# Attention and mixture of experts on one core: three PSUM banks shared in turn by scores and side work, a fourth bank for the maxima

## The chip, the cores and the metric

The kernel runs on one core of a Trainium2 chip. The metric is the device time of one execution in microseconds (us). TensorE is called PE below, its weight loads PEld, VectorE is DVE, ScalarE is ACT, GpSimd is POOL, and SyncE, which issues most transfers, is SP.

## What is computed

The input is 16 images of 128 channels and 32x32 pixels. Each image is normalised over its channels, goes through an attention of 8 heads of 16 features over 1024 tokens, is projected and added to the input. Then each token is normalised again and goes to the two best of 16 experts.

```python
xs = reshape(x, (B, T, C))                      # B = 16, T = 1024, C = 128
q, k, v = einsum('btc,hcd->bhtd', xs, Wq), ...  # H = 8 heads, D = 16
att = softmax(einsum('bhtd,bhsd->bhts', q, k) / sqrt(D))
x = x + reshape(concat_heads(att @ v) @ Wproj + bproj)
t = tokens(x)
t = t + experts(top2_gating(layernorm(t)))      # E = 16, capacity 256, hidden 512
```

## The kernel before

It has two phases. The attention of the 16 images takes the first three quarters of the time; then 272 blocks of 128 rows go through the experts. The change concerns the first phase.

**Slots.** An image is 128 slots. A slot is one matmul of scores, with 128 keys as rows and 512 queries as columns of one head (`score_unit`, L1515), and the exponential of that tile on ACT (`exp_unit`, L818). The softmax needs a row maximum before it. So every slot also has one matmul for the maxima (`max_unit`, L1491), with 128 queries as rows and 512 keys as columns, which DVE reduces along the row (`take_max`, L978). PE is 45 slots ahead with these (`LEAD`): in slot u it issues the maximum matmul of slot u + 45 and then the score matmul of slot u. An image has four stages of 32 slots. After the last maximum of a stage, DVE splits the 128x16 maxima into two parts, PE transposes them into rows (`rows_of_maxima`, L1501, in the slots with u % 32 == 24), ACT copies the rows out (L850), and two transfers put them below the queries, where the score matmul subtracts them.

**Weighing.** After every fourth score PE multiplies four finished probability tiles with the values (`weigh`, L1532, eight matmul instructions). It waits for the exponential of the last of the four. In a stage it comes after the scores of slots 2, 7, 10, 14, 18, 22, 26 and 30. At the end of a stage DVE divides the result in four small steps (slots 4 to 7 of the next stage); the first weighing of a stage, in slot 7, also waits for the first of them (L1010).

**Side work.** The order in which PE does the rest is written out by hand by the slot. For the image after: two groups of transposes of x (after the scores 1 and 5, L1463), four projections to queries and keys (33, 41, 44, 48, L1471), and two groups of projections to values (51, 54, L1477). For the image before: the output projection (13, 17, L1541), the transposes to tokens (20, 22, L1549), the gate's logits (36, L1556) and the token counts (77, L1565 to L1570). ACT reads most of these out of PSUM (L824, L836, L842, L855, L871), between its exponentials; DVE reads the output projection (`add_residual`, L1037) and the logits (`choose`, called in slot 38, L1058 and two more steps).

**PSUM.** There are eight banks of 128x512 values. Banks 0 to 2 are a ring for the scores, banks 3 to 5 a ring for the maxima, bank 6 takes the weighing, and bank 7, `misc`, takes all the side work: `misc_free` makes PE wait until the last thing in it has been read. In the last image the late side work goes to bank 4. PE runs its list in order, so a wait of one matmul holds all that stand behind it. The rings are numbered by the slot of the image, and 128 is not a multiple of 3, so the first two slots of an image wait for one item more than the others:

```python
def ring_free(n):
    return n - RING + 1 if n % SLOTS >= SLOTS % RING else n - SLOTS % RING + 1
...
wait(pe, exp_done, SLOTS * b + ring_free(u))       # score_unit
wait(pe, max_taken, SLOTS * b + ring_free(m))      # max_unit
```

Of the kernel before, what the change touches and what calls it, by code (L numbers as in the profile page):

```python
# [10 lines left out]
ACT = mybir.ActivationFunctionType  # L11
# [18 lines left out]
RING = 3  # L30
# [65 lines left out]
def ring_free(n):  # L96


    return n - RING + 1 if n % SLOTS >= SLOTS % RING else n - SLOTS % RING + 1

# [6 lines left out]
def metaformer(nc, x, wq, wk, wv, wproj, bproj, wgate, w1, w2, out):  # L107
    ctx = ExitStack()
    with ctx:
# [126 lines left out]
        def misc_of(b):  # L236
            return banks[:, 4] if b == B - 1 else misc
# [574 lines left out]
        def _(act):  # L812
            def exp_unit(b, u):

                wait(act, scores_ready, SLOTS * b + u + 1)
                if u % 4 == 0:
                    wait(act, pv_done, 32 * b + (u - PRING) // 4 + 1)
                nc.scalar.activation(probs[:, u % PRING, :], ps_score[:, u % RING, :], ACT.Exp,  # L818
                                     scale=SCALE).then_inc(exp_done, 1)

            def copy_xt(b, half):
# [3 lines left out]
                                     misc[:, :].rearrange("p (j c) -> p j c", j=4), ACT.Copy).then_inc(xt_copied, 1)  # L825

            def copy_qk(b, i):
# [8 lines left out]
                nc.scalar.activation(parts[:, o, 1, half * HALF:(half + 1) * HALF], misc[:, :],  # L836
                                     ACT.Copy).then_inc(qk_copied, 1)

            def copy_v(b, half):
# [3 lines left out]
                                     misc[:, :].rearrange("p (j n) -> p j n", j=4), ACT.Copy).then_inc(v_copied, 1)  # L843

            def copy_m(b, s):
# [4 lines left out]
                nc.scalar.activation(m_row[0:MROWS, :], misc[0:MROWS, :], ACT.Copy).then_inc(m_copied, 1)  # L850

            def copy_tokens(b, half):
# [3 lines left out]
                                     misc_of(b)[:, :].rearrange("p (j c) -> p j c", j=4), ACT.Copy).then_inc(tok_copied, 1)  # L856
# [11 lines left out]
            def copy_counts(b):  # L868
                wait(act, cs_psum, b + 1)
                wait(act, routed, b)  # L870
                nc.scalar.activation(counts[:, :], misc_of(b)[:, 0:TB * 3 * E + 3 * E], ACT.Copy).then_inc(cs_taken, 1)  # L871
# [99 lines left out]
        def _(dve):  # L971
            def take_max(b, m):
# [5 lines left out]
                nc.vector.tensor_reduce(out=m_red[:, s % 2, at:at + 1], in_=ps_max[:, m % SLOTS % RING, :], axis=AX.X,  # L978
# [54 lines left out]
            def add_residual(b, half):  # L1033
# [3 lines left out]
                nc.vector.tensor_tensor(out=x1[:, cols], in0=misc_of(b)[:, :], in1=res[:, cols],  # L1037
# [5 lines left out]
            def choose(b):  # L1043
# [14 lines left out]
                nc.vector.tensor_tensor(out=gat[:, :, :], in0=misc_of(b)[:, 0:TB * E].rearrange("p (j e) -> p j e", j=TB),  # L1058
# [219 lines left out]
            nc.vector.tensor_tensor(out=wg_c[:, :], in0=misc[:, 0:E], in1=wg_sb[:, :],  # L1278
# [20 lines left out]
            def batch(b, first, last):  # L1299
                for u in range(SLOTS):  # L1300
# [14 lines left out]
                    if not first:  # L1315
# [8 lines left out]
                        if u == 38:  # L1324
# [126 lines left out]
        def _(pe):  # L1451
            freed = [None]

            def misc_free(sem_, value):
                if freed[0] is not None:
                    pe.wait_ge(*freed[0])
                freed[0] = (sem_, value)

            def transpose_x(b, half):
                misc_free(xt_copied, 2 * b + half + 1)  # L1460
                wait(pe, x_loaded, 16 * (b + 1))
                for j in range(4):
                    last = nc.tensor.transpose(misc[:, j * P:(j + 1) * P],  # L1463
# [3 lines left out]
            def project_qk(b, i):  # L1467
                o, half = i // 2, i % 2
                misc_free(qk_copied, 4 * b + i + 1)
                wait(pe, xt_normed, TB * (b + 1))  # L1470
                nc.tensor.matmul(misc[:, :], wq_r[:, o, :], xt[:, 4 * half:4 * half + 4, :], start=True,  # L1471
                                 stop=True).then_inc(qk_psum, 1)

            def project_v(b, half):
                misc_free(v_copied, 2 * b + half + 1)
                for j in range(4):
                    last = nc.tensor.matmul(misc[:, j * P:(j + 1) * P], xt[:, 4 * half + j, :], wv_sb[:, :, :],  # L1477
# [3 lines left out]
            def max_unit(b, m):  # L1481
# [8 lines left out]
                wait(pe, max_taken, SLOTS * b + ring_free(m))  # L1490
                nc.tensor.matmul(ps_max[:, m % SLOTS % RING, :],  # L1491
# [4 lines left out]
            def rows_of_maxima(b, s):  # L1496
                k = STAGES * b + s
                misc_free(m_copied, k + 1)
                wait(pe, m_split, 2 * (k + 1))
                for t in range(4):  # L1500
                    last = nc.tensor.transpose(misc[0:MROWS, t * P:(t + 1) * P],  # L1501
# [3 lines left out]
            def score_unit(b, u):  # L1505
# [8 lines left out]
                wait(pe, exp_done, SLOTS * b + ring_free(u))  # L1514
# [227 lines left out]
```

## Time and profile before

| | |
|---|---|
| median of 3 runs | 2329.85 us (2327.37 to 2330.93) |
| profiled execution, first to last instruction | 2326.0 us |
| PE busy | 2117.5 us, 91% |
| DVE busy | 1840.5 us, 79% |
| ACT busy | 1544.5 us, 66% |
| POOL busy | 1046.1 us, 45% |
| first score matmul starts | 64.4 us |
| last score matmul starts | 1735.8 us |

The profiled execution has no time of its own beside its span; the span is 3.9 us, or 0.2%, below the median of the runs. Busy time is the union of an engine's instructions. A row of the timeline gives the start, the duration, the engine, the line, the operation, what it writes and reads, how many merged instructions it stands for, and in brackets the idle time of the engine before it and who ended it. A matmul's row lasts from its first column to its end in PSUM, so rows of matmuls overlap; the distance of two starts tells what one costs PE.

### The profile page before, as it was taken

To read this page: it belongs to the slowest core of one execution; us is meant where nothing else is said; L and a number is where in the kernel's file an instruction comes from. 1 tells how busy PE (TensorE), PEld (TensorE's weight loads), DVE (VectorE), ACT (ScalarE), POOL (GpSimd) and SP (SyncE) were. 2 spreads that over 40 slices of the span, in tenths; PEclk is the share of its full clock that TensorE was granted. 3 is DMA by queue.
4 is the path that set the end of the run, shared out by engine and by line. 5 is a ranking of instruction groups with operands and counts; after the bars stand their busy time and mean duration, and the time that the engine had idled before them with its cause. 6 is when DMAs were issued, how large, how long until landed. Compare 5 with 4: busy or idle time off the path is not lost. (4 is left out here: it accounts for less than half of the span.)

```text
span 2326.0 us, 48689 instructions
## 1 busy us (share of the span) xinstructions
PE 2117.5 (91%) x14610; PEld 1160.1 (50%) x14610; DVE 1840.5 (79%) x4370; ACT 1544.5 (66%) x3153; POOL 1046.1 (45%) x1650
## 2 busy tenths in 40 slices
PE   6989999998999999999989999999888999999996
PEld 3333333333333333333333333333328999999996
DVE  6899989899899989899898999999954544445564
ACT  1677777777776777767676767777664666556553
POOL 3203444443434444444534445444344577645442
PEclk9999999999999999999999999999998999999997
DMA  4222223231323233231323332232233222222576
GB/s 123 47 41 57 57 56 69 42 71 35 68 47 65 49 67 61 49 74 35 68 39 64 55 63 58 56 59 43 61 118 112 72 71 82 89 65 70 155 241 184
DMA packets 135676, 170.79 MB, mean 73 GB/s; under 512 B 31568, under 2 KB 101592, under 8 KB 135414
## 3 DMA queue, kind: packets, MB, share of 16 engines
q1 hardware_dynamic: 118582, 134.25, 26.7%
q0 software_dynamic: 16896, 34.12, 4.2%
q8 instruction: 97, 1.59, 0.3%
q14 instruction: 101, 0.83, 0.1%
HBM read 64.86 MB, written 48.87 MB: 49 GB/s over the span
## 5 line engine op out<-in xcount | busy, mean ns | idle before, releaser
L978 DVE TENSOR_REDUCE sb_m_red<-banks 128x1 f32<-128x512 f32 x2048 | 1326.4, 678 | 154.6 <-PE banks L1491 153.1
L818 ACT ACTIVATE sb_arena_a<-banks 128x512 f32<-128x512 f32 x2048 | 1114.7, 599 | 444.3 <-PE banks L1515 421.2
L1491 PE MATMUL banks<-sb_arena_b 62*128 62x512 f32 x2048 | 815.2, 468 | 104.6 <-DVE sb_m_red L978 91.8
L1515 PE MATMUL banks<-sb_arena_b 64*128 64x512 f32 x2048 | 807.6, 463 | 7.1 <-ACT sb_arena_a L818 7.0
L1491 PEld LDWEIGHTS banks<-sb_arena_b 62*128 62x128 f32 x2048 | 347.6, 188 | 770.7 <-DVE sb_m_red L978 658.1
L1532 PE MATMUL banks<-sb_arena_a,sb_arena_d 128*32 128x512 f32 x4096 | 552.2, 611 | 6.5 <-ACT sb_arena_a L818 0.7
L747 POOL DMA_INDIRECT sorted_rows<-sb_rows,sb_place x256 | 251.4, 982 | 349.0 <-PE banks L1515 318.1
L791 POOL DMA_INDIRECT expert_out<-sb_arena_d x272 | 272.0, 1000 | 240.1 <-DVE sb_arena_d L1368 178.1
L1515 PEld LDWEIGHTS banks<-sb_arena_b 64*128 64x128 f32 x2048 | 338.4, 186 | 28.4 <-ACT sb_arena_a L818 28.0
L1657 PE MATMUL banks<-sb_arena_d,sb_arena_c 128*128 128x128 f32 x2176 | 290.8, 277 | 0.5 <-DVE sb_arena_c L1358 0.5
L1666 PE MATMUL banks<-sb_arena_c 128*128 128x128 f32 x2176 | 288.3, 276 | 0.0
L1657 PEld LDWEIGHTS banks<-sb_arena_d,sb_arena_c 128*128 128x128 f32 x2176 | 267.6, 194 | 1.0 <-ACT sb_arena_d L925 0.8
L1666 PEld LDWEIGHTS banks<-sb_arena_c 128*128 128x128 f32 x2176 | 266.0, 193 | 0.0
L1361 DVE COPY sb_arena_c<-sb_arena_b 128x512 f32 x272 | 134.9, 496 | 165.5 <-PE banks L1666 162.3
L932 ACT ACTIVATE sb_arena_c<-banks 128x512 f32<-128x512 f32 x272 | 162.4, 597 | 112.7 <-PE banks L1657 110.9
L1358 DVE COPY sb_arena_c<-sb_arena_a 128x512 f32 x272 | 115.6, 425 | 79.7 <-issue 41.1
L939 ACT ACTIVATE sb_arena_d<-banks,sb_arena_d 128x128 f32<-128x128 f32 x272 | 99.9, 367 | 100.0 <-PE banks L1666 90.6
L1532 PEld LDWEIGHTS banks<-sb_arena_a,sb_arena_d 128*32 128x32 f32 x4096 | 81.0, 108 | 152.3 <-issue 69.4
L627 POOL TENSOR_SCALAR sb_arena_d<-sb_v_st 128x512 f32<-128x512 f32 x32 | 19.6, 615 | 273.3 <-PE banks L1532 256.6
L925 ACT ACTIVATE sb_arena_d<-banks 128x128 f32<-128x128 f32 x272 | 73.4, 270 | 35.6 <-PE banks L1649 35.1
L1649 PE MATMUL banks<-sb_ident,sb_arena_d 128*128 128x128 f32 x272 | 74.9, 276 | 18.4 <-DMA sb_arena_d<-sorted_rows 18.4
L1471 PE MATMUL banks<-sb_xt,sb_wq_r 128*128 128x512 f32 x128 | 75.9, 676 | 10.3 <-POOL sb_xt L609 8.2
(166 smaller groups left out, 1620.1 us busy)
## 6 DMA issues: line engine op xcount, KB each, us to landing
sb_arena_b<-sb_arena_c SPq DMA_DIRECT2D x768, 64.0 KB, 2.3
sb_arena_d<-sorted_rows SPq DMA_DIRECT2D x272, 66.0 KB
sb_x_in<-in_x_dram SPq DMA_DIRECT2D x16, 512.0 KB, 3.5
sb_res<-in_x_dram SPq DMA_DIRECT2D x16, 512.0 KB, 3.2
sb_x_all<-sb_res SPq DMA_DIRECT2D x16, 512.0 KB, 3.1
expert_out<-sb_arena_d POOLq DMA_INDIRECT x272
sorted_rows<-sb_rows,sb_place POOLq DMA_INDIRECT x256
sb_arena_a<-in_L_ffn_w_dram SPq DMA_DIRECT2D x4, 1024.0 KB, 7.1
```

The lines of the kernel that those rows point to most:

```text
L747: nc.gpsimd.indirect_dma_start(out=sorted_rows[:, :], out_offset=bass.IndirectOffsetOnAxis(ap=place[:, k, j:j + 1], axis=0), in_=rows[:, k ...
L791: nc.gpsimd.indirect_dma_start(out=expert_out[:, :], out_offset=bass.IndirectOffsetOnAxis(ap=blk_dest[:, s % WR:s % WR + 1], axis=0), in_= ...
L818: nc.scalar.activation(probs[:, u % PRING, :], ps_score[:, u % RING, :], ACT.Exp, scale=SCALE).then_inc(exp_done, 1)
L932: nc.scalar.activation(hid[:, s % 2, :], ps_h[:, s % 2, :], ACT.Relu).then_inc(hid_done, 1)
L978: nc.vector.tensor_reduce(out=m_red[:, s % 2, at:at + 1], in_=ps_max[:, m % SLOTS % RING, :], axis=AX.X, op=ALU.max).then_inc(max_taken, 1)
L1358: nc.vector.tensor_copy(w1_blk[:, s % WR, :], w1_all[:, bass.ds(e, 1), :].rearrange("p a h -> p (a h)")).then_inc(w1_copied, 1)
L1361: nc.vector.tensor_copy(w2_blk[:, s % WR, :], w2_all[:, bass.ds(e, 1), :, :].rearrange("p a c d -> p (a c d)")).then_inc(w2_copied, 1)
L1491: nc.tensor.matmul(ps_max[:, m % SLOTS % RING, :], qs[rows_of, g, l, half * HALF + t * P:half * HALF + (t + 1) * P], ks[rows_of, g, l, kh ...
L1515: nc.tensor.matmul(ps_score[:, u % RING, :], ks[rows_of, g, l, i * P:(i + 1) * P], qs[rows_of, g, l, half * HALF:(half + 1) * HALF], start ...
L1532: last = nc.tensor.matmul(ps_pv[32 * h:32 * h + 32, :], v_pad[:, i, HG * g + h, :], probs[:, (4 * n + h) % PRING, :], start=(i == 0), stop ...
L1657: last = nc.tensor.matmul(ps_h[:, s % 2, c * P:(c + 1) * P], w1_blk[:, s % WR, c * P:(c + 1) * P], blk_xt[:, s % 2, :], start=True, stop=True)
L1666: last = nc.tensor.matmul(ps_o[s % WR], hid[:, s % 2, c * P:(c + 1) * P], w2_blk[:, s % WR, c * P:(c + 1) * P], start=(c == 0), stop=(c == ...
```

## The change

The side work has no bank of its own any more. Everything that PE issues into the front banks 0 to 2 (scores, side work, the rows of maxima) is put in one list, `front_order`, and the n-th item gets bank n % 3. A matmul into a bank first waits for the reader of what was there before, the item three places earlier. Banks 3 to 6 are the ring of the maxima, now of four, and bank 7 takes the weighing. 128 is a multiple of 4, and the list of the front banks runs on over the end of an image, so `ring_free` goes. `choose` is called in slot 36 instead of 38, so that DVE reads the logits before PE needs their bank again. The slots of the side work stay as they are, and no matmul, copy or transfer is added or removed. Before the first image, one explicit wait for the small gate matrix stands where `misc_free` had it; before the experts, the wait is for the last readers of the three front banks.

```diff
-RING = 3
+FRONT, MRING = 3, 4
...
+XT_AT, QK_AT, V_AT = (1, 5), (33, 41, 44, 48), (51, 54)
+OUT_AT, TOK_AT, LOGITS_AT, COUNT_AT = (13, 17), (20, 22), 36, 77
...
+def front_order():
+    yield from (("xt", 0, 0), ("xt", 0, 1), ("wg", 0, 0))
+    yield from (("qk", 0, i) for i in range(4))
+    yield from (("v", 0, 0), ("v", 0, 1), ("m", 0, 0))
+    for b in range(B):
+        for u in range(SLOTS):
+            yield "score", b, u
+            if b < B - 1:
+                yield from (("xt", b + 1, i) for i, at in enumerate(XT_AT) if at == u)
+                yield from (("qk", b + 1, i) for i, at in enumerate(QK_AT) if at == u)
+                yield from (("v", b + 1, i) for i, at in enumerate(V_AT) if at == u)
+            if b > 0:
+                yield from (("out", b - 1, i) for i, at in enumerate(OUT_AT) if at == u)
+                yield from (("tok", b - 1, i) for i, at in enumerate(TOK_AT) if at == u)
+                if u == LOGITS_AT:
+                    yield "logits", b - 1, 0
+                if u == COUNT_AT:
+                    yield "counts", b - 1, 0
+            if u % UNITS == MSLOT and not (b == B - 1 and u > 96):
+                yield ("m", b, u // UNITS + 1) if u // UNITS + 1 < STAGES else ("m", b + 1, 0)
...
+FRONT_BANK = {what: n % FRONT for n, what in enumerate(front_order())}
...
-        ps_score, ps_max = banks[:, 0:RING], banks[:, RING:2 * RING]
-        ps_pv, misc = banks[:, 6], banks[:, 7]
+        ps_max, ps_pv = banks[:, FRONT:FRONT + MRING], banks[:, FRONT + MRING]
...
-                        if u == 38:
+                        if u == LOGITS_AT:
                             choose(b - 1)
...
-            freed = [None]
-            def misc_free(sem_, value):
-                if freed[0] is not None:
-                    pe.wait_ge(*freed[0])
-                freed[0] = (sem_, value)
+            freed = [None] * 8
+            def take(bank, sem_, value):
+                if freed[bank] is not None:
+                    wait(pe, *freed[bank])
+                freed[bank] = (sem_, value)
+            def take_front(what, b, i, sem_, value):
+                take(4 if b == B - 1 and what in LATE else FRONT_BANK[what, b, i], sem_, value)
+                return front(what, b, i)
...
-                wait(pe, max_taken, SLOTS * b + ring_free(m))
-                nc.tensor.matmul(ps_max[:, m % SLOTS % RING, :],
+                wait(pe, max_taken, SLOTS * b + m - MRING + 1)
+                nc.tensor.matmul(ps_max[:, m % MRING, :],
...
-                wait(pe, exp_done, SLOTS * b + ring_free(u))
-                nc.tensor.matmul(ps_score[:, u % RING, :], ks[rows_of, g, l, i * P:(i + 1) * P],
+                to = take_front("score", b, u, exp_done, SLOTS * b + u + 1)
+                nc.tensor.matmul(to, ks[rows_of, g, l, i * P:(i + 1) * P],
...
+            pe.wait_ge(setup_v, 12)
...
-            pe.wait_ge(m_copied, STAGES * B)
+            for bank in range(FRONT):
+                wait(pe, *freed[bank])
```

## Rows read from the trace of the kernel before

**Rows 1.** Busy time by windows, two images: stretch, length, engines, PEclk, DMA.
```profile
1325.20:1430.10 104.90, 95.88 (x620) 37.80 (x616) 96.04 (x214) 77.06 (x146) 47.94 (x86) 1.00 0.29 57
1007.30:1113.30 106.00, 97.42 (x620) 38.15 (x617) 96.11 (x214) 77.04 (x146) 47.80 (x85) 0.98 0.28 57
```

**Rows 2.** Page, costliest groups: busy, mean ns, idle before and its releaser.
```profile
L978 DVE TENSOR_REDUCE sb_m_red<-banks 128x1 f32<-128x512 f32 x2048 | 1326.4, 678 | 154.6 <-PE banks L1491 153.1
L818 ACT ACTIVATE sb_arena_a<-banks 128x512 f32<-128x512 f32 x2048 | 1114.7, 599 | 444.3 <-PE banks L1515 421.2
```

**Rows 3.** Busy time by windows, slots 62 to 77 of the image from 1325.2.
```profile
1380.20:1393.05 12.85, 10.94 (x69) 3.66 (x67) 12.85 (x34) 9.61 (x19) 2.95 (x2) 1.00 0.35 57
```

**Rows 4.** Timeline, one plain group of four slots, from weighing to weighing.
```profile
1405.93 1.06 PE L1532 MATMUL banks<-sb_arena_a,sb_arena_d 128*32 128x512 f32 x8
...
1407.46 2.48 DVE L978 TENSOR_REDUCE sb_m_red<-banks 128x1 f32<-128x512 f32 x4 [0.22 <-PE banks L1491]
1407.49 2.06 ACT L818 ACTIVATE sb_arena_a<-banks 128x512 f32<-128x512 f32 x4 [0.64 <-PE banks L1515]
...
1408.21 0.49 PE L1491 MATMUL banks<-sb_arena_b 62*128 62x512 f32 x1 [0.32 <-DVE sb_m_red L978]
...
1408.63 1.06 PE L1532 MATMUL banks<-sb_arena_a,sb_arena_d 128*32 128x512 f32 x8
```

**Rows 5.** Timeline of PE in the last image, where no maxima are left.
```profile
1729.57 1.07 PE L1532 MATMUL banks<-sb_arena_a,sb_arena_d 128*32 128x512 f32 x8
...
1731.75 0.49 PE L1515 MATMUL banks<-sb_arena_b 64*128 64x512 f32 x1 [0.45 <-ACT sb_arena_a L818]
1732.17 1.07 PE L1532 MATMUL banks<-sb_arena_a,sb_arena_d 128*32 128x512 f32 x8
```

**Rows 6.** Timeline where an image begins.
```profile
1325.19 0.63 PE L1491 MATMUL banks<-sb_arena_b 62*128 62x512 f32 x2
...
1325.42 1.78 ACT L818 ACTIVATE sb_arena_a<-banks 128x512 f32<-128x512 f32 x3 [0.64 <-PE banks L1515]
...
1326.07 0.50 PE L1515 MATMUL banks<-sb_arena_b 64*128 64x512 f32 x1 [0.24 <-ACT sb_arena_a L818]
```

**Rows 7.** Timeline, slots 33 to 42 of the image from 1325.2.
```profile
1353.82 0.50 PE L1491 MATMUL banks<-sb_arena_b 62*128 62x512 f32 x1 [0.21 <-DVE sb_m_red L978]
...
1356.55 1.68 POOL L602 TENSOR_TENSOR sb_rstd<-sb_ln_var,sb_neg_half 128x8 f32<-128x8 f32 x1
...
1357.40 1.96 PE L1556 MATMUL banks<-sb_wg_c,sb_res 128*128 128x16 f32 x16
...
1359.82 0.69 DVE L978 TENSOR_REDUCE sb_m_red<-banks 128x1 f32<-128x512 f32 x1 [0.64 <-PE banks L1491]
...
1361.57 0.28 DVE L1058 TENSOR_TENSOR sb_gat<-banks,sb_rstd 128x128 f32<-128x128 f32 x1
...
1363.35 0.50 PE L1491 MATMUL banks<-sb_arena_b 62*128 62x512 f32 x1 [0.33 <-DVE sb_m_red L978]
```

**Rows 8.** Timeline, slots 51 to 54: first projection to values and its copy.
```profile
1372.00 1.16 PE L1477 MATMUL banks<-sb_wv_sb,sb_xt 128*128 128x128 f32 x8
...
1373.66 0.39 PE L1515 MATMUL banks<-sb_arena_b 64*128 64x512 f32 x1
...
1374.15 0.59 ACT L842 ACTIVATE sb_v_st<-banks 128x512 f32<-128x512 f32 x1
```

**Rows 9.** Timeline, slot 74.
```profile
1390.84 0.50 PE L1491 MATMUL banks<-sb_arena_b 62*128 62x512 f32 x1 [0.43 <-DVE sb_m_red L978]
```

**Rows 10.** Timeline, slot 110.
```profile
1417.33 0.50 PE L1491 MATMUL banks<-sb_arena_b 62*128 62x512 f32 x1
```

**Rows 11.** Timeline, slots 119 to 122: exponentials of 119 and 120, maximum of 122.
```profile
1424.73 1.09 ACT L818 ACTIVATE sb_arena_a<-banks 128x512 f32<-128x512 f32 x2 [0.64 <-PE banks L1515]
...
1425.71 0.40 PE L1491 MATMUL banks<-sb_arena_b 62*128 62x512 f32 x1
```

**Rows 12.** Timeline before the first image: second projection.
```profile
21.63 2.07 PE L1471 MATMUL banks<-sb_xt,sb_wq_r 128*128 128x512 f32 x2 [0.69 <-ACT sb_arena_c L836]
```

More of the change, by code:

```diff
@@ L232, in metaformer, with front @@
         banks = ctx.enter_context(nc.psum_tensor("banks", [P, 8, HALF], FP32))
-        ps_score, ps_max = banks[:, 0:RING], banks[:, RING:2 * RING]
-        ps_pv, misc = banks[:, 6], banks[:, 7]
-        def misc_of(b):
-            return banks[:, 4] if b == B - 1 else misc
+        ps_max, ps_pv = banks[:, FRONT:FRONT + MRING], banks[:, FRONT + MRING]
+        def front(what, b, i=0):
+            return banks[:, 4] if b == B - 1 and what in LATE else banks[:, FRONT_BANK[what, b, i]]
         ps_h, ps_xt = banks[:, 0:2], banks[:, 6:8]
@@ L817, in exp_unit @@
                     wait(act, pv_done, 32 * b + (u - PRING) // 4 + 1)
-                nc.scalar.activation(probs[:, u % PRING, :], ps_score[:, u % RING, :], ACT.Exp,
+                nc.scalar.activation(probs[:, u % PRING, :], front("score", b, u), ACT.Exp,
                                      scale=SCALE).then_inc(exp_done, 1)
@@ L824, in copy_xt @@
                 nc.scalar.activation(xt[:, 4 * half:4 * half + 4, :],
-                                     misc[:, :].rearrange("p (j c) -> p j c", j=4), ACT.Copy).then_inc(xt_copied, 1)
+                                     front("xt", b, half).rearrange("p (j c) -> p j c", j=4),
+                                     ACT.Copy).then_inc(xt_copied, 1)
             def copy_qk(b, i):
@@ L842, in copy_v @@
                 nc.scalar.activation(v_st[:, 4 * half:4 * half + 4, :, :].rearrange("p j h d -> p j (h d)"),
-                                     misc[:, :].rearrange("p (j n) -> p j n", j=4), ACT.Copy).then_inc(v_copied, 1)
+                                     front("v", b, half).rearrange("p (j n) -> p j n", j=4),
+                                     ACT.Copy).then_inc(v_copied, 1)
             def copy_m(b, s):
@@ L855, in copy_tokens @@
                 nc.scalar.activation(tok[:, 4 * half:4 * half + 4, :],
-                                     misc_of(b)[:, :].rearrange("p (j c) -> p j c", j=4), ACT.Copy).then_inc(tok_copied, 1)
+                                     front("tok", b, half).rearrange("p (j c) -> p j c", j=4),
+                                     ACT.Copy).then_inc(tok_copied, 1)
             def gate_exponentials(b):
@@ L870, in copy_counts @@
                 wait(act, routed, b)
-                nc.scalar.activation(counts[:, :], misc_of(b)[:, 0:TB * 3 * E + 3 * E], ACT.Copy).then_inc(cs_taken, 1)
+                nc.scalar.activation(counts[:, :], front("counts", b)[:, 0:TB * 3 * E + 3 * E], ACT.Copy).then_inc(cs_taken, 1)
             copy_xt(0, 0)
@@ L1036, in add_residual @@
                 wait(dve, res_ready, b + 1)
-                nc.vector.tensor_tensor(out=x1[:, cols], in0=misc_of(b)[:, :], in1=res[:, cols],
+                nc.vector.tensor_tensor(out=x1[:, cols], in0=front("out", b, half), in1=res[:, cols],
                                         op=ALU.add).then_inc(x1_ready, 1)
@@ L1590, in batch @@
             def batch(b, first, last):
-                freed[0] = (m_copied, STAGES * b + 1)
                 for u in range(SLOTS):
```

92 lines of the change are left out of this document (39 added, 53 removed).

## The prediction

> **What bounds the kernel now.** I read the page first. On it DVE's maxima and ACT's exponentials are the costliest groups, and nearly all of DVE's idle time before a maximum, 153.1 of 154.6 us, ends when PE delivers the matmul [rows 2]. Then the windows of one image: in 104.9 us both PE (95.88) and DVE (96.04) are busy for over nine tenths, ACT for 77.06 [rows 1]. So neither is the bound throughout; they hold each other up through the ring of the maxima. The timeline shows where. In slots 62 to 77 DVE has extra work and no idle time, and PE waits for it [rows 3]. In slots 33 to 61 PE has the projections, the logits and the transposes, and DVE starves [rows 7]. In the plain slots both wait a little: a group of four takes 2.70 us from weighing to weighing; DVE's four maxima take 2.48 us with 0.22 us of idle time ahead, and the last of PE's four maximum matmuls is held for DVE at 1408.21 [rows 4].
>
> The plain group has a second limit, of which the waits say nothing, because it is only just covered. The first score after a weighing is read by ACT from 1407.49, for 0.60 us [rows 2, 4]; so its bank comes free at 1408.09, and the fourth score, which needs it, starts 0.12 us later. The last image shows this limit by itself: no maxima are left, the fourth score waits for ACT, and a group still takes 2.60 us (1729.57 to 1732.17) [rows 5]. A longer ring for the maxima can therefore take no more than 0.10 us from a plain group. I take 0.06, since after 1408.09 some 0.05 us pass before PE starts.
>
> **What the change gives, per image.** Times are those of the image from 1325.2; a quiet image repeats them closely.
>
> The numbering over the seam. Slots 0 and 1 wait for one exponential more than the rest. The score of slot 1 starts at 1326.07, just after the exponential of slot 127 (from 1325.42, 0.60 us) has ended, and the row names ACT as releaser [rows 2, 6]. Without this it would start one pair of matmuls, 0.34 us, after the maximum ahead of it at 1325.19, so at 1325.53 [rows 6]. Gain 0.53 us. DVE starves in slots 2 and 3, so PE's time counts in full.
>
> The fourth bank of the maxima gains where PE waits for DVE and then has a stretch with long side work. In slot 33 PE waited 0.21 us of engine idle time and started 0.27 us later than a pair's distance [rows 7]; with the 0.07 of the group before, 0.34. In slot 42 it waited 0.33 us, because DVE was at `choose` (1361.57) [rows 7]. There two things help: the ring, and `choose` in slot 36, where DVE now idles 0.64 us (to 1359.82) while PE works on the logits for 1.96 us from 1357.40. What `choose` needs from POOL is done at 1358.23, before the logits are, so the earlier call waits for nothing new [rows 7]. If POOL were late, DVE would stand in slot 36 for as long. Gain 0.40. In slot 74 PE waited 0.43 us, plus what a pair costs [rows 9]; I take 0.54 for the entry to slot 77, below the 0.62 that one reduction takes back to back (a quarter of 2.48) [rows 4]. In slot 110 the last pair started at 1417.33; the score could start 0.35 us earlier, when its bank mate's exponential has ended [rows 10]. Seven plain groups gain 0.06 each, 0.42. Sum of the gains: 0.53 + 0.34 + 0.40 + 0.54 + 0.35 + 0.42 = 2.58 us.
>
> **What it costs, per image.** Now the side work stands between the scores in three banks, and the score three places after it waits for its reader. Walking the list of the front banks against the times of before, I find most mates long free, because a weighing of 1.0 us [rows 4] or another side item lies between. One is not. After the first projection to values (slot 51) come the scores 52, 53 and 54 and only then a weighing. Score 54 gets the projection's bank. It started at 1373.66; ACT copies the projection after the exponential of slot 52, from 1374.15 to 1374.74 [rows 8]. So score 54, and behind it the weighing, the second projection and all that follows, start at 1374.79: 1.13 us late. This lies in the stretch where DVE starves, so nothing hides it.
>
> The rows of the maxima in slots 88 and 120 push each following score to a later mate. Score 122 now waits for the exponential of slot 120, which ends at 1425.82; its pair started at 1425.71 [rows 11]. It starts at 1425.87, 0.16 late; twice, 0.32. In slots 24 and 56 the rows of the maxima wait for the copy three places before as they do now, which costs nothing new. Slots 22, 47 and 51 have mates released close to the start; I allow 0.2 us for the three, an estimate. The transposes in slot 5 are held about 0.3 us for the exponential of slot 3; DVE is the bound from there to slot 22, and the weighing of slot 7 waits for DVE's transpose anyway, so I cost it at nothing; without that cover it would be 0.3. The output projection's banks are read by DVE before PE is back at them. Sum of the costs: 1.13 + 0.32 + 0.20 = 1.65 us.
>
> Net 0.93 us per image, 15 images: 14 us. The last image has no projections; it keeps a plain gain of about 0.5.
>
> **The start.** The projections of the first image alternated with their copies in one bank: each began 0.69 us after PE had finished the one before [rows 12]. With three banks they follow one another. The keys, on which the first maxima wait, are the fourth: three gaps, 2.1 us. All else shifts with them.
>
> **Sum.** 14 + 0.5 + 2.1 = 16.6 us off the span of 2326.0, so 2309.4; the median of the runs is 3.9 above the profiled execution, so 2313. The experts' phase is not touched.
>
> **Bounds.** Below: if the front bank waits cost nothing, 15 x 1.65 = 25 us more would be gained, 2288. And DVE's busy time of 96.04 of 104.9 us is the floor of an image: 15 x 8.9 = 133 us, out of reach with the wait in slot 54. Above: if the fourth bank gains nothing (slots 33, 42, 74, 110 and the plain groups, 2.05 us), an image is 1.12 us longer: 15 x 1.12 - 2.6 = 14 us slower, 2344.
>
> **A rule against it.** The clock row first: quiet images have PEclk 1.00 and take 104.9 us, others have 0.98 and take 106.0 [rows 1], because the clock fell from 2.4 to 1.2 GHz for a few us of them. Eight of the fourteen middle images are quiet. The Trainium skill ("TensorE: Matmul & The Clock Gate", A second HAM failure mode: psum-queue depth-cycling) tells of a kernel whose cycling through the PSUM banks left short idles that made the clock swing between its levels. By that rule the wait of 1.13 us before the score of slot 54 is one more such idle. The same skill ("Perfetto Trace Analysis", Matmuls) wants independent groups to rotate through banks so that the reading of one overlaps the next, and by that alone the change is right. As a mechanism of this kernel: if the half speed came in every image, those eight would each pay 1.1 us [rows 1], 9 us, and the time would be 2322.
>
> **The rivals.**
> 1. The score ring is the limit and the fourth bank is idle (slower). Place: the plain groups and slots 74 and 110, where the exponential three places back frees the bank 0.12 us before its score. For it: [rows 4, 5]. Against: in slots 74 and 42 the rows name DVE as releaser of 0.43 and 0.33 us [rows 7, 9]. It decides once the fourth bank gives under 1.12 us per image. Time 2334 to 2344.
> 2. The gains are larger: PE's lead of one more maximum survives from stretch to stretch, and the plain groups run at DVE's pace. Then half of DVE's idle time, 4.4 us per image, goes, 66 us, and with the start the time is 2261; anything from there to 2300 counts here. Against: slot 54, and the 2.60 us of [rows 5].
> 3. Gains and costs cancel, 2325 to 2334: the wait in slot 54 takes what the seam and slots 33 to 77 give.
> 4. More half-speed stretches, 2322 as above.
>
> **Chances.** The forecast, 2300 to 2325: 0.50. Rival 1: 0.17. Rival 2: 0.12. Rival 3: 0.13. Rival 4: 0.08. What a measurement of this kernel can tell from no change is about 0.2%, 4.7 us. Faster: 0.50 + 0.12 + 0.08 = 0.70; the same 0.13; slower 0.17. The likeliest case's own range is 2300 to 2325. The range for 8 in 10 runs from 2295, which leaves out nearly all of rival 2, to 2338, which leaves out about half of rival 1.
>
> **What would show it.** The profile after should have: score 54 and the weighing behind it held for ACT's copy L842 (now without any wait), some 1.1 us in 15 images; no wait for ACT at the second score of an image; plain groups of 2.64 us, with ACT instead of DVE as the releaser of the fourth pair; DVE's idle time per image about as now less 1 us; the logits' read L1058 one maximum ahead of where it stood; images of about 104 us; and the first score of the first image some 2 us earlier. The prediction is wrong if images stay at 104.9 or over with the wait in slot 54 as sized (then the fourth bank gives nothing), or if that wait is absorbed and images come near 102.

## The result, and the profile after

| | before | after |
|---|---|---|
| median of the runs | 2328.6 us (2326.4 to 2330.9, 4 runs) | 2372.2 us (2368.0 to 2374.8, 4 runs) |
| profiled execution, first to last instruction | 2326.0 us | 2368.4 us |
| mean granted clock of TensorE | 0.984 | 0.958 |
| first score starts | 64.4 us | 60.8 us |
| from there to the first score of the last image | 1575.5 us | 1622.8 us |
| last image, first score to last | 95.9 us | 94.4 us |

The ratio is 1.0192 (1.0174 to 1.0211): the changed kernel is slower by 1.9%, where 0.7% faster was forecast, and it lies outside the range. The start came out better than forecast (3.6 us earlier, forecast 2.1) and so did the last image. The images between are 47.4 us longer, fifteen of them, 3.2 us each; that is more than the whole loss.

The page's costliest groups of the changed kernel (busy us, mean ns, idle us before and its releaser) answer to [rows 2]:

```profile
L1009 DVE TENSOR_REDUCE sb_m_red<-banks 128x1 f32<-128x512 f32 x2048 | 1321.5, 677 | 177.8 <-PE banks L1527 173.7
L846 ACT ACTIVATE sb_arena_a<-banks 128x512 f32<-128x512 f32 x2048 | 1113.2, 599 | 486.8 <-PE banks L1551 469.4
L1551 PE MATMUL banks<-sb_arena_b 64*128 64x512 f32 x2048 | 800.8, 467 | 20.3 <-ACT sb_v_st L871 11.1
L1527 PE MATMUL banks<-sb_arena_b 62*128 62x512 f32 x2048 | 759.1, 459 | 50.9 <-DVE sb_m_red L1009 38.6
```

DVE now idles 177.8 us before its maxima (154.6 before). The waits view says that PE's wait for them has shrunk as meant, though the longest single one has grown, and that PE now waits for two other things. The view of before first (us in total, times, longest):

```profile
PE banks L1491 <- DVE sb_m_red L978: 91.8, 295, 1.3
```

and of after:

```profile
PE banks L1527 <- DVE sb_m_red L1009: 38.6, 52, 1.8
...
PE banks L1568 <- DVE sb_o_t L1041: 13.8, 32, 0.7
PE banks L1551 <- ACT sb_v_st L871: 11.1, 15, 0.7
```

The wait of L1551 for the copy is the one forecast for slot 54. The weighing's wait for DVE's transpose (L1041) stood before only at its weight loads, 20.5 us in 47 waits. So the fourth bank works: 52 waits in place of 295. Yet an image is longer. Busy time by windows of the changed kernel, the image that answers to the one in [rows 1] and two stretches inside it (stretch, length, PE, PEld, DVE, ACT, POOL, PEclk, DMA share, GB/s):

```profile
1358.50:1467.80 109.30, 101.78 (x618) 41.23 (x616) 97.45 (x214) 77.00 (x146) 48.05 (x86) 0.95 0.28 55
1419.00:1425.00 6.00, 3.74 (x20) 1.22 (x19) 6.00 (x11) 3.49 (x7) 2.94 (x2) 0.86 0.48 77
1425.00:1430.50 5.50, 5.07 (x24) 1.23 (x23) 4.89 (x13) 2.68 (x5) 0.00 (x0) 0.53 0.22 36
```

109.3 us in place of 104.9, with the clock at 0.95 over the image and 0.53, so mostly at 1.2 of 2.4 GHz, for 5.5 us of it. The timeline just ahead of that stretch (slots 68 to 71) shows the place:

```profile
1420.60 0.62 POOL L655 TENSOR_SCALAR sb_arena_d<-sb_v_st 128x512 f32<-128x512 f32 x1 [13.15 <-PE banks L1568]
...
1420.82 0.43 DVE L1154 TENSOR_TENSOR sb_masks<-sb_masks,sb_small 128x8 f32<-128x8 f32 x1
...
1421.16 0.68 DVE L1009 TENSOR_REDUCE sb_m_red<-banks 128x1 f32<-128x512 f32 x1
1421.19 2.35 POOL L661 TENSOR_TENSOR sb_res<-sb_res,sb_bias 128x1024 f32<-128x1024 f32 x1
1421.76 1.81 DVE L1157 TENSOR_TENSOR sb_masks<-sb_masks,sb_small 128x8 f32<-128x8 f32 x1
...
1421.89 0.50 PE L1527 MATMUL banks<-sb_arena_b 62*128 62x512 f32 x1 [0.43 <-DVE sb_m_red L1009]
...
1424.22 0.79 PE L1527 MATMUL banks<-sb_arena_b 62*128 62x512 f32 x1 [1.83 <-DVE sb_m_red L1009]
...
1425.44 1.94 PE L1568 MATMUL banks<-sb_arena_a,sb_arena_d 128*32 128x512 f32 x8 [0.43 <-DVE sb_o_t L1041]
```

L1157 is one of DVE's small steps of the choice of experts, 128x8 elements, and takes 1.81 us. It ends at 1423.57; POOL's addition of the bias, L661, has run from 1421.19 to 1423.54. L1154 is held in the same way by L655 (0.43 us, to 1421.25, against 1421.22). Behind L1157 wait two maxima, and behind these PE, 1.83 us; its next matmuls take 0.79 and the weighing 1.94, against 0.50 and 1.06. It is so in all fourteen middle images: L1157 takes 1.80 to 1.81 us in the first fourteen of its sixteen uses, and 0.16 in the last two. The trace of before holds the same thing twice, in rows that the prediction did not use:

```profile
1368.26 0.62 POOL L617 TENSOR_SCALAR sb_arena_c<-sb_arena_c 128x512 fp32r<-128x512 f32 x1 [1.17 <-ACT sb_arena_c L836]
...
1368.33 0.69 DVE L1085 TENSOR_TENSOR sb_gat<-sb_tmp,sb_small 128x128 f32<-128x128 f32 x1
...
1370.33 0.28 DVE L1093 TENSOR_TENSOR sb_tmp<-sb_gat,sb_small 128x128 f32<-128x128 f32 x1
...
1385.71 0.17 DVE L1123 TENSOR_TENSOR sb_masks<-sb_masks,sb_small 128x8 f32<-128x8 f32 x1
...
1386.12 0.62 POOL L627 TENSOR_SCALAR sb_arena_d<-sb_v_st 128x512 f32<-128x512 f32 x1 [12.51 <-PE banks L1532]
...
1386.38 0.38 DVE L1126 TENSOR_TENSOR sb_masks<-sb_masks,sb_small 128x8 f32<-128x8 f32 x1
1386.68 1.27 DVE L978 TENSOR_REDUCE sb_m_red<-banks 128x1 f32<-128x512 f32 x2
1386.71 2.36 POOL L633 TENSOR_TENSOR sb_res<-sb_res,sb_bias 128x1024 f32<-128x1024 f32 x1
```

L1085 and L1093 have the same shape and two inputs from SBUF; under L617 the one takes 0.69 us, and with POOL at rest the other 0.28. L1126 took 0.38 under L627 (it ends at 1386.76, L627 at 1386.74), and had begun 0.33 us before the addition L633 did. L978, which reads PSUM and has one input, is not held: two of them take 1.27 us under L633. The Trainium skill ("SBUF — State Buffer", SBUF: two separate sides) says that a VectorE instruction with two SBUF inputs and a GpSimd instruction that reads SBUF exclude each other for the whole of whichever began first. These rows agree for the side they show, DVE held by POOL: the 128x8 steps end within 0.03 us of POOL's instruction.

The table compares the kernels by stretches of slots. For each slot it takes the distance from the start of its score matmul to that of the next, the median of that over the fourteen middle images, and subtracts the same of before; a row is the sum over its slots, in us. "Later addition" and "earlier choice, slot 52" are experiments below.

| slots | after | later addition | earlier choice, slot 52 | what lies there |
|---|---|---|---|---|
| 0 to 3 | -0.42 | -0.43 | -0.43 | seam |
| 4 to 27 | +0.09 | +0.09 | +0.10 | DVE's statistics, projections out |
| 28 to 35 | -0.24 | -0.24 | -0.24 | slot 33 |
| 36 to 43 | +0.86 | -0.41 | -0.43 | logits, `choose` |
| 44 to 51 | +0.11 | +0.10 | -1.11 | slot 51's projection gone in the last |
| 52 to 55 | +1.24 | +1.24 | +1.27 | slot 54; in the last, slot 52's projection |
| 56 to 67 | -0.63 | -0.61 | -0.61 | plain groups, slots 64 to 67 |
| 68 to 75 | +3.94 | +1.13 | -0.66 | L1157 under POOL; slot 71 |
| 76 to 127 | -0.51 | -0.52 | -0.42 | plain groups, slots 90, 110, 122 |

They sum to +4.44, +0.35 and -2.55 us per image. A sum of medians counts what most images do; the mean image changes by +3.30, +0.57 and -2.97. For the changed kernel most of the difference lies in slots 36 to 43. There the granted clock fell in six of the fourteen images before and in nine after, so the median steps from one kind of image to the other, while the mean grows by only 0.10. In slots 68 to 75 the means are +3.49 and +1.01. The medians show where something happens, the means what it costs.

The clock in slots 71 to 79 parts the kernels more sharply. It was below full speed there in no middle image before, in all fourteen after the change, in ten with the later addition and in none with the earlier choice.

### The profile page after: what moved, and what is told of

Read it like the earlier page. It is cut to its first block and busy times, and to the rows that moved or that the text cites. A ratio compares the mean times of both kernels' runs of the same rounds, so it can differ in the third digit from the quotient of the medians.

```text
span 2368.4 us, 48690 instructions
## 1 busy us (share of the span) xinstructions
PE 2181.6 (92%) x14610; PEld 1209.7 (51%) x14610; DVE 1859.8 (79%) x4370; ACT 1543.5 (65%) x3153; POOL 1048.0 (44%) x1650
## 5 line engine op out<-in xcount | busy, mean ns | idle before, releaser
L1009 DVE TENSOR_REDUCE sb_m_red<-banks 128x1 f32<-128x512 f32 x2048 | 1321.5, 677 | 177.8 <-PE banks L1527 173.7
L1551 PE MATMUL banks<-sb_arena_b 64*128 64x512 f32 x2048 | 800.8, 467 | 20.3 <-ACT sb_v_st L871 11.1
L1527 PE MATMUL banks<-sb_arena_b 62*128 62x512 f32 x2048 | 759.1, 459 | 50.9 <-DVE sb_m_red L1009 38.6
L1568 PE MATMUL banks<-sb_arena_a,sb_arena_d 128*32 128x512 f32 x4096 | 572.3, 632 | 14.5 <-DVE sb_o_t L1041 13.8
L1551 PEld LDWEIGHTS banks<-sb_arena_b 64*128 64x128 f32 x2048 | 340.8, 189 | 130.5 <-ACT sb_arena_a L846 89.6
L655 POOL TENSOR_SCALAR sb_arena_d<-sb_v_st 128x512 f32<-128x512 f32 x32 | 19.6, 615 | 268.2 <-PE banks L1568 259.4
```

The costliest lines, as they stand in the source:

```text
L1527: nc.tensor.matmul(ps_max[:, m % MRING, :], qs[rows_of, g, l, half * HALF + t * P:half * HALF + (t + 1) * P], ks[rows_of, g, l, kh * HALF: ...
L1551: nc.tensor.matmul(to, ks[rows_of, g, l, i * P:(i + 1) * P], qs[rows_of, g, l, half * HALF:(half + 1) * HALF], start=True, stop=True).then ...
L1568: last = nc.tensor.matmul(ps_pv[32 * h:32 * h + 32, :], v_pad[:, i, HG * g + h, :], probs[:, (4 * n + h) % PRING, :], start=(i == 0), stop ...
```

## The experiments

Each ran against the kernel before on the same chip, whose median was 2327.1, 2326.7 and 2326.6 us in the three groups. Ratios are to it, taken over all runs, so they can differ from the ratio of the medians by up to 0.0006.

### Is it POOL's addition? Five kernels

**a_bias**, the changed kernel with the addition put off:

```diff
 def add_bias(b):
     wait_apart(gp, gp_passed, res_loaded, 16 * (b + 1))
+    wait(gp, scores_ready, SLOTS * b + 77)
```

> The changed kernel, with one edit: POOL's addition of the bias (L661, 2.35 us) waits until 77 scores of the image are issued, so that it no longer runs when DVE does its small steps on the masks. Theory A (collision): in slots 66 to 75 of the changed kernel DVE's step on 128x8 elements takes 1.81 us instead of 0.38, because it starts inside POOL's addition and ends with it; PE then waits 1.83 us, and the clock falls there. By A the 3.9 us that slots 68 to 75 lost per image come back: 14 x 3.9 = 55 us, so about 2317 us (2310 to 2325), and that step takes 0.2 us. Theory B (the waits of the shared banks themselves, slot 54 above all, cost the time and bring the clock down): no change, 2365 to 2375.

Measured: 2328.3 us (2322.6 to 2337.6, 10 runs), ratio 1.0001 (0.9987 to 1.0015). **b_bias**, the same line in the kernel before.

> The kernel before, with the same edit of POOL's addition of the bias. Theory A: there the step just precedes the addition and takes 0.38 us; without any overlap it takes 0.16, 3 us over all images, so 2325 to 2330. Theory B: 2329. It shows that what the edit gives in the changed kernel is not a gain of the edit by itself.

Measured: 2325.6 us, ratio 1.0000 (0.9990 to 1.0011). So one wait on POOL is worth 44 us after the change and nothing clear of noise before it. Theory B of a_bias is out; theory A's range ended at 2325, since it gave back all 3.9 us of slots 68 to 75, of which the table leaves 1.1. In the timeline of a_bias the last step is short; L1155 is still held by the placing of the values:

```profile
1389.38 0.62 POOL L655 TENSOR_SCALAR sb_arena_d<-sb_v_st 128x512 f32<-128x512 f32 x1 [13.18 <-PE banks L1569]
...
1389.57 0.45 DVE L1155 TENSOR_TENSOR sb_masks<-sb_masks,sb_small 128x8 f32<-128x8 f32 x1
...
1390.54 0.15 DVE L1158 TENSOR_TENSOR sb_masks<-sb_masks,sb_small 128x8 f32<-128x8 f32 x1
```

**b_hit** does the reverse: nothing of the change, but the addition over DVE's steps.

```diff
 def add_bias(b):
     wait_apart(gp, gp_passed, res_loaded, 16 * (b + 1))
+    wait(gp, scores_ready, SLOTS * b + 67)
...
-                    place_v(b + 1, 0)
-                add_bias(b)
+                add_bias(b)
+                if not last:
+                    place_v(b + 1, 0)
```

> The old kernel, with nothing of the change in it; only GpSimd's addition of the bias (2.36 us) is put ahead of its placing of the values and started when the score of slot 66 is done, so that it lies over VectorE's last 128x8 steps of the masks. Theory A (a VectorE tensor_tensor with two SBUF inputs stands still until GpSimd's instruction over it has ended, and that makes the change slow): one of the steps L1120, L1123, L1126 takes 1 to 2 us in place of 0.17 to 0.38, TensorE waits for the maxima behind it in slots 68 to 75, the clock falls there in most images, an image grows by 1.5 to 4 us, and the time is 2350 to 2390 us. Theory B (the loss comes from the bank waits of the change, the addition only goes along with it): the steps or the image don't change, 2324 to 2334 us.

Measured: 2352.0 us, ratio 1.0116 (1.0097 to 1.0136). Its timeline, and the windows view of one image of it:

```profile
1397.57 2.36 POOL L634 TENSOR_TENSOR sb_res<-sb_res,sb_bias 128x1024 f32<-128x1024 f32 x1 [11.49 <-PE banks L1517]
1398.16 1.79 DVE L1125 TENSOR_TENSOR sb_masks<-sb_masks,sb_small 128x8 f32<-128x8 f32 x1
...
1400.60 0.49 PE L1493 MATMUL banks<-sb_arena_b 62*128 62x512 f32 x1 [1.55 <-DVE sb_m_red L980]
```

```profile
1337.60:1443.90 106.30, 95.88 (x618) 37.78 (x617) 97.47 (x215) 77.23 (x146) 47.99 (x86) 1.00 0.28 56
```

The same held step (it ends at 1399.95, the addition at 1399.93), in a kernel that has none of the change: theory A holds, and theory B is out. It also parts the two costs. In eight of the fourteen middle images the clock stayed at full speed here (the one shown has PEclk 1.00), and slots 68 to 71 grew by 1.42 us: the hold alone. In the other six it fell and slots 68 to 75 took 0.3 to 0.8 us more. In the changed kernel the clock falls in all fourteen. In five of them it does so only behind slot 71: slots 68 to 71 take 5.76 us against 4.10 in those images of a_bias where the clock stays, 1.66 us for the hold, and slots 72 to 75 take 3.76 against 2.22, 1.54 us for PE at the lower level of 1.2 GHz. In the other nine it falls earlier and slots 68 to 75 take up to 1.0 us more again. That the clock falls in most images was expected of b_hit and did not come.

**a_mask** leaves POOL alone and moves DVE's steps; **b_mask** is the same edit in the kernel before.

```diff
-                        if u == 41:
+                        if u == 38:
                             gate_exponentials(b - 1)
...
-                        if u == 44:
+                        if u == 40:
                             choice = choose_experts(b - 1)
-                        if u >= 44 and u % UNITS not in BUSY:
+                        if u >= 40 and u % UNITS not in BUSY:
```

> The changed kernel, GpSimd's order as it is; instead ScalarE takes the gates' exponential in slot 38 (was 41) and VectorE begins the choice of experts in slot 40 (was 44), so that the last two-input step comes in slot 62 (was 66), ahead of GpSimd's placing and addition. Theory A: the 1.8 us step is gone without a wait on GpSimd, and since VectorE also has less to do in slots 64 to 71, the weighing of slot 71 is less late: 2318 to 2330 us. Theory B (loss from the bank waits): the time stays at 2365 to 2380 us. Rival to both: the steps in slots 40 to 49 meet GpSimd's splitting of queries and keys instead (0.62 and 1.27 us), hold VectorE there, and it is 2330 to 2350 us.

> The old kernel with only the choice of experts begun in slot 40 and the gates' exponential in slot 38. It asks what of the 62 us between the changed kernel and its version with this edit is the removed collision, and what the edit gives by itself. Theory A (the edit gives VectorE room in slots 64 to 77 also in the old kernel, where TensorE waits for it): 2312 to 2322 us. Rival (the old kernel never had the collision, and its ring of three gains nothing from the room): 2324 to 2330 us.

Measured: a_mask 2310.0 us, ratio 0.9937 (0.9915 to 0.9960), below its theory A's range; b_mask 2313.8 us, ratio 0.9948 (0.9933 to 0.9963). The edit is worth 62 us after the change and 13 before it. Of the 13 most are room for DVE in slots 64 to 79, where [rows 3] show it full: those slots are 0.84 us shorter, and 40 to 43 are 0.25 longer; the rest is that the clock fell behind the logits in three images instead of six. The other 49 fit the collision, found a second way, with the falls of the clock in slots 68 to 79, of which a_mask has none; a_bias gave 44 and kept ten of the falls.

### Is the wait of slot 54 sized right? Two kernels

**a_v52** in the changed kernel, and **a_mask_v52**, the same on top of a_mask:

```diff
-XT_AT, QK_AT, V_AT = (1, 5), (33, 41, 44, 48), (51, 54)
+XT_AT, QK_AT, V_AT = (1, 5), (33, 41, 44, 48), (52, 54)
...
-                        if u == 52:
+                        if u == 53:
                             copy_v(b + 1, 0)
```

> The changed kernel, with the first projection to values one slot later (after score 52 instead of 51, its copy after exponential 53), so that the weighing of slot 54 lies between it and the score that takes its bank. Theory A: the wait of 1.13 us per image goes (17 us), the collision stays: 2350 to 2360. Theory B: with the longest wait for a shared bank gone the clock stays up too, and the time comes to within 10 us of the kernel before, 2320 to 2340.

> As a_mask, and the first projection to values moves from slot 51 to 52, its copy from 52 to 53, so that no score waits for the copy. Theory A (the wait of slot 54 costs 1.13 us per image, as the prediction had it): 15 to 20 us below a_mask, 2300 to 2313 us, faster than the kernel before. Rival (VectorE or the clock takes it back in slots 56 to 77): within 5 us of a_mask.

The timeline of the changed kernel, slots 53 and 54, and the next maximum:

```profile
1408.02 0.59 ACT L871 ACTIVATE sb_v_st<-banks 128x512 f32<-128x512 f32 x1
...
1408.67 0.49 PE L1551 MATMUL banks<-sb_arena_b 64*128 64x512 f32 x1 [0.73 <-ACT sb_v_st L871]
...
1411.71 0.69 DVE L1009 TENSOR_REDUCE sb_m_red<-banks 128x1 f32<-128x512 f32 x1 [1.97 <-PE banks L1527]
```

Measured: a_v52 2352.2 us, ratio 1.0114 (1.0096 to 1.0132), 20 us below the changed kernel, as theory A had it; a_mask_v52 2284.2 us (2281.3 to 2285.2), ratio 0.9823 (0.9809 to 0.9838), 26 us below a_mask. Per image that is 1.3 and 1.7 us; by slots the move of the projection takes 1.2 us out (103.56 to 102.32 us between the first scores of two images, median), where 1.13 was forecast. The 26 us of a_mask_v52 are more than its range had: besides the move, the clock fell in three middle images of a_mask and in none of a_mask_v52, and its last image is 2.7 us shorter. DVE does not take it back there. a_mask_v52 is the best version found, 1.8% below the kernel before. Windows view of one of its images, and its group of the maximum matmuls (idle before, releasers):

```profile
1286.80:1389.10 102.30, 97.58 (x618) 40.55 (x616) 95.52 (x215) 76.58 (x146) 48.30 (x86) 1.00 0.30 59
```

```profile
L1527 PE MATMUL banks<-sb_arena_b 62*128 62x512 f32 x2048 | 737.7, 448 | 19.9 <-DMA sb_arena_b<-sb_arena_c 9.0 <-DVE sb_m_red L1009 6.2
```

PE waits only 6.2 us in all for the maxima. In a_mask_v52 other steps of the choice are held under POOL's splitting of queries and keys:

```profile
1329.56 1.27 POOL L648 TENSOR_TENSOR sb_arena_c<-sb_arena_c 128x512 fp32r<-128x512 f32 x1
1330.08 0.90 DVE L1134 TENSOR_TENSOR sb_masks<-sb_tmp,sb_small 128x128 f32<-128x128 f32 x1
```

That is the rival written down for a_mask, and it happens: 0.90 us in place of 0.28. It costs nothing there: in a_mask DVE is held twice in slots 44 to 51 (0.67 and 0.90 us), in the changed kernel once (0.69), and these slots take 0.12 and 0.11 us more than before. DVE starves in these slots. So what a hold costs depends on who waits behind DVE, and not on its length alone.

### What do the ring, the seam and the logits give by themselves? Three kernels

**a_ring3** is the changed kernel with three banks for the maxima (bank 6 unused):

```diff
-FRONT, MRING = 3, 4
+FRONT, MRING = 3, 3
...
-        ps_max, ps_pv = banks[:, FRONT:FRONT + MRING], banks[:, FRONT + MRING]
+        ps_max, ps_pv = banks[:, FRONT:FRONT + MRING], banks[:, 7]
...
```

and the maximum's bank is that of `(SLOTS * b + m) % MRING`.

> The changed kernel with three instead of four banks for the maxima; one bank lies idle. Only the sharing, the numbering over the image's end and the earlier read of the logits are left of the change. Theory A: DVE lags PE by one maximum less, so its small steps come before POOL's addition as in the kernel before, and the collision is gone; what the sharing costs (1.65 us per image) less seam and logits (0.53 + 0.2) gives 2335 to 2350, faster than the full change. Theory B: the waits for the shared banks stay and the fourth bank's gain is missing, 2370 to 2400.

Measured: 2346.8 us, ratio 1.0086 (1.0069 to 1.0103). It is in theory A's range. Slots 68 to 75 differ from before by 0.00 and the clock falls in none of them: without the fourth bank the step that was held takes 0.37 to 0.38 us, as before. Slot 54 costs its 1.24 us and the seam gives 0.43. With the collision put aside the fourth bank is worth 18 us, with all that the clock does (2346.8 against 2328.3 of a_bias). PE waits for the maxima as before:

```profile
PE banks L1526 <- DVE sb_m_red L1008: 90.9, 289, 0.5
```

**b_seam** is the kernel before with both rings numbered on over the seam (`ring_free(n)` returns `n - RING + 1`, and the bank is that of `SLOTS * b + u`). **b_choose** is the kernel before with `choose` in slot 36.

> The old kernel with only the numbering of the two rings continued from image to image. Theory A (the first term of the prediction, 0.53 us per image, measured as 0.43 in the slots 0 to 3 of the changed kernel): 2319 to 2323 us. Rival (what the seam gives is given back at the next place where VectorE is the bound, slots 8 to 22): 2325 to 2330 us, with slots 0 to 3 shorter by 0.4 and slots 4 to 23 longer by as much.

> The old kernel with only the reading of the logits on VectorE moved from slot 38 to 36. The prediction gave slot 42 a gain of 0.40 us, from this and the fourth bank together, without parting them. Theory A (it is this move that takes VectorE's delay of 0.33 us from slot 42): slots 40 to 43 shorter by 0.3 to 0.4 us and the time 2320 to 2324 us. Rival (it is the fourth bank, or a fall of the clock behind the logits takes it back): 2325 to 2330 us.

Measured: b_seam 2311.2 us, ratio 0.9941 (0.9922 to 0.9959); b_choose 2322.5 us, ratio 0.9985 (0.9976 to 0.9995). The seam alone gives 0.75 us in slots 0 to 3, more than the 0.53 of the prediction and the 0.43 of the changed kernel, where the transposes in slot 1 now wait 0.26 us for an exponential. The rest of the 15 us, which put the time below both ranges written down for it, lies in slots 36 to 39, 0.39 us per image in the mean and 0.00 in the median: the clock falls behind the logits in one middle image instead of six. No run shows why. `choose` alone gives slots 40 to 43 only 0.11 of the 0.40 booked; the median of the later-addition kernel, with the fourth bank, is 0.41 there, and a_ring3, without it, gains 0.11. So the fourth bank gives most of it, and the time of b_choose lies in theory A's range for another reason: the clock fell in three images instead of six.

### Two attempts at a better version

**b_seam_mask** is b_seam with the edit of b_mask, no banks shared. **a_mask_v52_m26** is a_mask_v52 with the transposes of the rows of maxima behind the weighing of slot 26:

```diff
-MSLOT = 24
+MSLOT = 26
```

> The old kernel with the continued numbering and the earlier choice: the best that was found without sharing banks. The two parts lie in other slots, so they should add: 2298 to 2308 us. If it comes at or below 2290 us, sharing the banks and the fourth bank of the maxima give nothing that the old layout can't have; the changed kernel with the earlier choice and the later projection took 2284 us.

> The best version so far, and the transposes of the rows of maxima go from slot 24 of a stage to slot 26, behind the weighing, so that no score has to wait for the exponential two places before it. Theory A (the 0.27 us that slots 88 and 120 gained in length are such waits, twice per image, as the prediction had them with 0.16 each): 8 us less, 2274 to 2280 us. Rival (the row of maxima then comes too late through its two transfers for the first score of the next stage, some 2 us of margin): a new wait of TensorE on a transfer at slots 0, 32, 64 and 96, 2285 to 2310 us.

Measured: b_seam_mask 2302.9 us, ratio 0.9898 (0.9883 to 0.9913). The two parts add for the most part (15.5 and 12.8 us alone, 23.7 together), and the time is in its range. The layout with shared banks and a fourth bank for the maxima is another 19 us better, once slot 51 and the choice are moved. a_mask_v52_m26: 2363.9 us, ratio 1.0167 (1.0148 to 1.0185), a miss by both theories' numbers. The timeline of its slots 27 to 29:

```profile
1484.89 0.57 ACT L880 ACTIVATE sb_m_row<-banks 8x512 f32<-8x512 f32 x1
...
1485.51 0.51 PE L1551 MATMUL banks<-sb_arena_b 64*128 64x512 f32 x2 [0.73 <-ACT sb_m_row L880]
```

Three front items behind the transposes comes the score of slot 29, with no weighing between; it waits for ACT's copy, and slots 28 to 31 of each of the four stages take 1.36 us longer than in a_mask_v52. It is the mistake of slot 54 again, which walking the list, as the prediction did, would have shown. The rival's wait for the transfers is there too, but small: 16.7 us in 63 waits, 0.27 us each.

## Why the prediction was wrong

By its own steps:

- **Bounds of the kernel before; start; tail.** Right. The start gave 3.6 us for 2.1: the four projections of queries and keys ran on without a gap, and the copies behind them moved too.
- **The seam, 0.53.** 0.43 in the changed kernel. It missed that slot 1's transposes wait, and called those of slot 5 free; they cost 0.12 there and slots 4 to 27 balance.
- **Slots 33 and 42, 0.34 and 0.40.** 0.24 in the changed kernel, and 0.41 in a_bias, in the medians. In the changed kernel the clock falls behind the logits in nine images instead of six, and in the mean slots 36 to 43 gain nothing (+0.10).
- **Plain groups 0.06; slot 110, 0.35.** 0.06 to 0.07, and 0.60. The weighings of two plain groups are 2.64 us apart, as forecast:

```profile
1441.62 1.07 PE L1568 MATMUL banks<-sb_arena_a,sb_arena_d 128*32 128x512 f32 x8
...
1444.26 1.06 PE L1568 MATMUL banks<-sb_arena_a,sb_arena_d 128*32 128x512 f32 x8
```

- **Slot 54, 1.13.** 1.24 in the slots, 1.2 by taking it out. Slots 90 and 122: 0.27 each for 0.16.
- **Slot 74 to 77, "I take 0.54".** This is the step that failed. It took DVE's work in slots 62 to 77 as fixed and only let PE run further ahead of it, so the sum has no term for DVE held by POOL. But PE also sets when POOL starts: POOL's placing and addition wait for a weighing. With a fourth bank PE stands one maximum further ahead of DVE, so POOL's 2.35 us begin earlier in DVE's list, 0.57 us before L1157 where they had begun 0.33 us after it. DVE's step has two SBUF inputs and stands until POOL is done. In place of a gain of 0.54 us, slots 68 to 75 take 3.49 us more in the mean. The size was right for what it looked at: in the four middle images of a_bias where the clock stays, slots 64 to 79 take 12.76 us against 13.28 before, 0.52 less. PE gains 0.54 of that in slots 64 to 67, waits again for DVE's transpose L1042 before the weighing of slot 71, and makes most of that up in 72 to 75. In the other ten images the clock falls behind this wait and the same slots take 14.2 us.
- **The rule against it, and rival 4.** The granted clock did fall more: 0.958 over the span, and 0.967 in the profiled execution without the collision. The windows view of a_bias shows one such fall, behind the weighing of slot 71:

```profile
328.00:330.00 2.00, 1.28 (x6) 0.37 (x4) 2.00 (x6) 1.93 (x5) 0.07 (x1) 1.00 0.56 92
330.00:332.00 2.00, 1.37 (x8) 0.20 (x8) 2.00 (x5) 0.57 (x1) 0.00 (x0) 0.61 0.56 94
332.00:334.00 2.00, 2.00 (x11) 0.83 (x7) 1.39 (x3) 0.64 (x2) 0.00 (x0) 0.54 0.04 10
```

The direction is that of the rule that the prediction cited from the Trainium skill ("TensorE: Matmul & The Clock Gate", A second HAM failure mode: psum-queue depth-cycling). Rival 4 sized it at 9 us and placed it at slot 54, where the windows show PEclk 1.00 (1406 to 1412 us, and in every middle image). It falls behind DVE's held step instead, or behind the late weighing of slot 71. What decides whether the clock falls is not settled: in b_hit it stayed in eight of fourteen images and in a_bias in four, and the waits of PE in slots 68 to 71 are the same where it stayed and where it fell (1.56 and 0.18 us in b_hit; 0.46, 0.18 and 0.72 in a_bias).
- **Rival 1** gave a slower time, 2334 to 2344, by another mechanism, which a_ring3 and the count of waits exclude: the fourth bank does give. Its price for a fourth bank that gives nothing, 2344, is what a_ring3 measures without one, 2346.8: the costs of sharing were sized about right. No rival named the collision, so the 0.17 for slower covers the direction and not the cause. The prediction said it would be wrong if images stayed at 104.9 or over, "then the fourth bank gives nothing"; they did, and it does.

Without the collision the change measures as no change, and here the profile says why the forecast gain is missing. Two of a_bias's middle images run at full clock throughout and take 104.1 us, against 104.9 for the quiet images before:

```profile
584.50:688.50 104.00, 97.99 (x618) 40.51 (x616) 95.33 (x214) 76.89 (x146) 48.02 (x85) 1.00 0.28 58
```

That is 0.8 us less, where 0.93 was forecast. The others pay for falls of the clock, above all the ten with one behind slot 71, where slots 68 to 75 take 7.8 to 7.9 us against 6.3. In its profiled execution, which lies 5.6 us above the median of its runs, the fifteen images come out 9.2 us longer, less 3.5 at the start and 1.6 in the last image. So two things stood between the forecast and the measured time: the hold, and the falls of the granted clock that went with it and partly stayed without it.

## What to carry to other kernels

Before letting one engine run further ahead, list what it triggers on a third engine and lay those instructions against the second engine's list; look for instructions of one line, or one shape, with two durations in the trace of before (0.28 and 0.69 us here), for they name the collision that is waiting. When a buffer ring is shared among kinds of work, walk the list of its items and ask of each whether the reader of the item one ring length before is quick; a slow reader (a copy queued behind an exponential) costs a whole wait wherever no long instruction lies between. A loss of 1.9% here hid a layout that is 1.8% faster than before, two small moves in time away. And compare images of one kind with each other, full clock with full clock, before a stretch is said to gain nothing.

## What the hardware did that was not expected

- A 128x8 `tensor_tensor` on DVE with two SBUF inputs takes 0.15 to 0.17 us alone and 1.79 to 1.81 us when POOL has just begun a 2.36 us addition; reductions of PSUM beside it keep their 0.68 us.
- One such hold of 1.8 us per image cost 1.42 us per image at full clock (b_hit). In the changed kernel, where the granted clock fell in every image with it (0.53 over 5.5 us in the one shown), slots 68 to 75 take 2.5 us more in the mean than in a_bias.
- The clock fell in slots 71 to 79 in all fourteen middle images of the changed kernel, in ten of a_bias, in six of b_hit and in none of before, a_ring3, a_mask and a_mask_v52.
